# An attention and feed-forward kernel on one core: a written-out order for the first bodies on every engine, one semaphore for each batch's row maxima, and the adapter's first product in two column halves

## What is computed

```python
# layer 0: cross attention (16 heads of 16), masked, then a feed-forward net with ternary weights
q, k, v = norm(x) @ w_q + b_q, ctx @ w_k + b_k, ctx @ w_v + b_v
x = x + (softmax(mask(q k^T / 4)) v) @ w_o + b_o
x = x + relu(norm(x) @ Wq1 + b1) @ Wq2 + b2          # Wq = clip(round(W / mean|W|), -1, 1)
# layer 1: cross attention with valid lengths, then experts
x = x + (softmax(pad(q k^T / 4)) v) @ W_o.T
h = norm(x)                                            # for each of 8 experts: reconstruct h
e = argmin over experts of sum((relu(h @ Wd1[e]) @ Wd2[e] - h)^2)     # one expert for each batch
y = x + h @ W_base + relu(h @ Wa_down[e] + ba_down[e]) @ Wa_up[e] + biases
```

## Time and profile before

| | us |
|---|---|
| median of 3 runs | 1704.53 |
| lowest, highest | 1703.83, 1711.43 |
| the profiled execution: its time | 1706.53 |
| the profiled execution: its span, first to last instruction | 1704.7 |

### The profile page before, as it was taken

One profiled execution on the slowest core, in us unless ns is written; L12 is line 12 of the kernel. 1 busy time (PEld: TensorE's weight loads), 2 busy tenths in 40 slices (PEclk: granted clock), 3 DMA queues, 4 the chain that ended last, 5 costly groups with the idle time before them and its releaser, 6 DMA issues.

```text
span 1704.7 us, 43831 instructions
## 1 busy us (share of the span) xinstructions
PE 1554.4 (91%) x15136; PEld 1282.7 (75%) x15136; DVE 1271.5 (75%) x5086; ACT 912.5 (54%) x2465; POOL 1098.4 (64%) x1198
## 2 busy tenths in 40 slices
PE   2567999999999999999999999999999999999875
PEld 1356788888888887888888888888888888877654
DVE  6446778888777788887777888877777888876542
ACT  0133556655555566555555566555555665555532
POOL 4377777666667766667677766666677667666200
PEclk7689999999999999999999999999999999999977
DMA  8446565656566655565666555556656565643311
GB/s 194 77 74 90 83 101 98 96 95 95 96 105 96 107 94 96 94 91 95 104 104 99 95 96 99 92 94 102 106 92 103 95 96 96 94 77 55 54 29 31
DMA packets 286212, 157.23 MB, mean 92 GB/s; under 512 B 38820, under 2 KB 281640, under 8 KB 285992
## 3 DMA queue, kind: packets, MB, share of 16 engines
q1 hardware_dynamic: 285992, 154.44, 56.0%
HBM read 111.36 MB, written 41.96 MB: 90 GB/s over the span
## 4 chain that ended last, share of the span: by engine, by line
PE 45%; DVE 24%; DMA 12%; issue 9%; SPq 7%; POOL 2%; ACT 1%; POOLq 0%; DVEq 0%; ACTq 0%
DMA qs<-scr 10%; DVE dif L924 7%; DVE dump L858 7%; PE psD L1234 6%; PE psD L1223 6%; SPq L375 4%; PE psS L1165 4%; PE psD L1202 4%; PE psD L1139 4%; PE psD L1268 3%; PE psD L1215 3%; PE psX L1177 3%; PE psD L1244 3%; SPq L359 2%; PE psV L1190 2%
## 5 line engine op out<-in xcount | busy, mean ns | idle before, releaser
L629 ACT ACTIVATE pT<-psX 128x512 f32<-128x512 f32 x512 | 304.9, 595 | 289.4 <-PE psX L1177 289.2
L522 POOL TENSOR_TENSOR pT<-pT,keep 128x512 f32<-128x512 f32 x256 | 318.6, 1271 | 5.5 <-ACT pT L629 5.5
L507 POOL TENSOR_SCALAR xn<-xr,mv,rstd 128x256 f32<-128x256 f32 x256 | 311.4, 1224 | 10.1
L481 POOL TENSOR_SCALAR veps<-mv 128x2 f32<-128x2 f32 x128 | 29.2, 228 | 405.6 <-DVE mv L803 403.1
L1165 PE MATMUL psS<-ks,qs 65*128 65x128 f16 x2048 | 203.4, 222 | 68.4 <-DMA qs<-scr 50.4
L850 DVE TENSOR_REDUCE mx<-psS 128x4 f32<-128x512 f32 x256 | 173.9, 679 | 119.4 <-PE psS L1165 119.4
L858 DVE CUSTOM_DVE_ANT_0 dump<-psS,bias 128x128 bf16<-128x128 f32 x1024 | 234.1, 285 | 34.2 <-PE psS L1165 31.6
L673 ACT ACTIVATE dif<-dif 128x256 f32<-128x256 f32 x512 | 208.6, 411 | 49.8 <-DVE dif L924 47.9
L924 DVE SCALAR_TENSOR_TENSOR dif<-psD,bd2s,xT 128x256 f32<-128x256 f32 x512 | 213.7, 471 | 21.1 <-PE psD L1244 21.1
L1177 PE MATMUL psX<-qs,ks 67*128 67x128 f16 x2048 | 199.7, 219 | 28.8 <-DMA qs<-mrows 18.5
L1165 PEld LDWEIGHTS psS<-ks,qs 65*128 65x128 f16 x2048 | 136.8, 98 | 114.9 <-issue 70.6
(11 more groups left out here) (103 smaller groups left out, 3006.7 us busy)
## 6 DMA issues: line engine op xcount, KB each, us to landing
scr<-packed SPq DMA_DIRECT2D x128, 256.0 KB, 2.4
ks<-scr SPq DMA_DIRECT2D x256, 128.0 KB, 5.3
qs<-scr SPq DMA_DIRECT2D x256, 128.0 KB, 4.4
adapter<-in_adapters SPq DMA_DIRECT2D x64, 192.5 KB, 3.7
xr<-in_x SPq DMA_DIRECT2D x32, 256.0 KB, 2.8
ctxT<-in_ctx SPq DMA_DIRECT2D x32, 256.0 KB, 3.0
qs<-mrows SPq DMA_DIRECT2D x512, 2.0 KB
out_y<-xr SPq DMA_DIRECT2D x32, 256.0 KB, 7.2
```

What stands on the lines that cost most here:

```text
L507: nc.gpsimd.tensor_scalar(xn[:, XN[s], b], xr[:, p % NX, b], mv[:, s, b, 0:1], rstd[:, s, b:b + 1], ALU.subtract, ALU.mult).then_inc(norme ...
L522: nc.gpsimd.tensor_tensor(blk, blk, keep[:, p % 2, j // 4].unsqueeze(1).to_broadcast([P, 4, P]), ALU.mult).then_inc(masked.sem, 1)
L629: nc.scalar.activation(pT[:, j], X[:], ACT.Exp, scale=SCALE).then_inc(exp_done[l].sem, 1)
```

## The change

**The slots.** A body has 96 slots instead of 16, so that each call has a slot of its own, and the loops begin at slot 220 (2.3 bodies). What comes before, the head, is written out call by call on each engine. Behind the head the order on each engine is the one of before, with one exception: `down` stands ahead of `scores_t(0, p, 5)` instead of behind `scores(1, p, 3)`, and `a_relus` ahead of `exps(0, p, 5)` instead of behind it. The waits of `normalise` and `exps` for who used their buffer last no longer come from a formula: they look into a table `holder` of the last user.

**The semaphores.** `m_landed` becomes one for each batch.

**The product.** `down` takes 64 of the adapter's columns instead of 128 (the upper 64 held nothing that was read), and the second batch's result goes to partitions 64 to 127. `a_relus` reads it there.

```diff
-BODY = 16
-LATE_SLOT = -4
-GAMMA_SLOT = -6
-QUANT_SLOT = -2
-FIRST = -14
-END = BODY * (NP - 1) + 83
+BODY = 96
+HEAD_END = 220
+TAIL_BEGIN = BODY * (NP - 1) + 462
...
-        m_landed = [sem(f"m_landed{l}") for l in range(2)]
+        m_landed = [[sem(f"m_landed{l}{b}") for b in range(PB)] for l in range(2)]
...
@@ SyncE
+            load_late(0)
...
+            load_late(13)
+            spill(0, 1, 0)
+            load_late(14)
+            load(2)
+            stack(0, 1, 0)
+            spill(0, 0, 0)
+            spill(0, 1, 1)
+            stack(0, 0, 0)
+            stack(0, 1, 1)
+            load(3)
...
@@ GpSimd
-                if s in (0, 1):
-                    T_ready[s + 2].done(pool, p - 3)
-                    T_ready[s].done(pool, p - 1)
-                else:
-                    T_ready[s - 2].done(pool, min(p + 2, NP - 1))
-                    T_ready[s].done(pool, p - 1)
+                if (XN[s], b) in holder:
+                    stage, pair = holder[XN[s], b]
+                    T_ready[stage].done(pool, pair)
+                holder[XN[s], b] = (s, p)
...
+            mask_parts(0)
+            mask_bias(0)
+            rstd_of(0, 0)
+            normalise(0, 0, 0)
+            normalise(0, 0, 1)
+            weight_sums()
+            mask_parts(1)
+            add_bias(0, 0)
...
+            rstd_of(1, 0)
+            normalise(1, 0, 0)
+            normalise(1, 0, 1)
+            apply_mask(1, 1)
+            apply_mask(1, 2)
+            apply_mask(1, 3)
+            add_bias(1, 0)
+            h_lows(0, 0)
+            apply_mask(1, 4)
+            h_lows(0, 1)
+            h_lows(0, 2)
+            h_lows(0, 3)
...
@@ ScalarE
-                    nc.scalar.activation(aT[0:R, b * P:b * P + P], bank["down"][0:R, b * P:b * P + P], ACT.Relu,
-                                         bias=adapter[0:R, b, AW - 1:AW]).then_inc(a_relu.sem, 1)
+                    nc.scalar.activation(aT[0:R, b * P:b * P + P], bank["down"][R * b:R * b + R, b * P:b * P + P],
+                                         ACT.Relu, bias=adapter[R * b:R * b + R, b, AW - 1:AW]).then_inc(a_relu.sem, 1)
...
@@ VectorE
+            statistics(0, 0)
+            any_of(0)
+            weight_parts()
+            length_rows()
+            any_rows(0)
+            low(0, 1, 0)
+            statistics(0, 1)
+            quantise_all()
+            low(0, 0, 0)
...
@@ TensorE
-                for b in range(PB):
-                    for k in range(KD):
-                        ins = nc.tensor.matmul(dst[:, b * P:b * P + P], adapter[:, b, k * R:k * R + P],
+                for k in range(KD):
+                    for b in range(PB):
+                        ins = nc.tensor.matmul(dst[R * b:R * b + R, b * P:b * P + P], adapter[:, b, k * R:k * R + R],
                                                xT3[:, p % 2, k, b * P:b * P + P], start=(k == 0), stop=(k == KD - 1))
```

More of the change, by code:

```diff
@@ new lines, in _ @@
+            load_late(14)
[6 more added lines that the diff above has]
+            load(3)
+            spill(0, 1, 2)
+            spill(0, 0, 1)
+            stack(0, 1, 2)
+            stack(0, 0, 1)
+            maxima(0, 0, 0)
+            maxima(0, 0, 1)
+            maxima(0, 1, 0)
+            spill(0, 0, 2)
+            stack(0, 0, 2)
+            spill(1, 1, 0)
+            maxima(0, 1, 1)
@@ L406, in _ @@
                     store(p)
-                for p in at(t, 51):
+                for p in at(t, 287):
                     maxima(1, p, 1)
[L409 to L434, removed]
@@ L532, in _ @@
                     normalise(2, p, 0)
-                for p in at(t, 33):
+                for p in at(t, 186):
                     normalise(2, p, 1)
[L535 to L561, removed]
@@ L966, in _ @@
             dve.wait_ge(consts_ready, 4)
-            for t in range(FIRST, END):
-                for p in at(t, 64):
+            statistics(0, 0)
[7 more added lines that the diff above has]
+            low(0, 0, 0)
+            any_of(1)
+            low(0, 1, 1)
+            any_rows(1)
+            values0(0)
+            low(0, 1, 2)
+            statistics(0, 2)
@@ L1276, in _ @@
             pe.wait_ge(bq_steps, 9)
-            for t in range(FIRST, END):
-                for p in at(t, 64):
-                    reconstruct(p, 1)
+            keys(0, 0)
+            count(0)
+            values(0, 0)
+            turn(0, 0)
+            keys(0, 1)
+            queries(0, 0)
+            count(1)
+            keys(0, 2)
+            values(0, 1)
+            turn(0, 1)
+            queries(0, 1)
+            scores(0, 0, 0)
+            scores(0, 0, 1)
+            count(2)
@@ new lines, in _ @@
+            turn(0, 2)
+            scores(0, 0, 2)
+            scores(0, 0, 3)
+            scores(0, 0, 4)
+            scores(0, 0, 5)
+            scores(0, 0, 6)
+            scores(0, 0, 7)
+            scores_t(0, 0, 0)
+            scores(0, 1, 0)
+            scores_t(0, 0, 1)
+            scores_t(0, 0, 2)
+            scores(0, 1, 1)
+            scores_t(0, 0, 3)
+            scores(0, 1, 2)
+            scores_t(0, 0, 4)
+            scores(0, 1, 3)
+            scores_t(0, 0, 5)
@@ new lines, in _ @@
+            mix(0, 0, 0)
+            scores_t(0, 0, 6)
+            scores(0, 1, 4)
+            scores_t(0, 0, 7)
+            scores(0, 1, 5)
+            scores_t(0, 1, 0)
+            mix(0, 0, 1)
+            scores(0, 1, 6)
+            queries(0, 2)
+            output(0, 0)
+            keys(1, 0)
+            scores(0, 1, 7)
+            scores_t(0, 1, 1)
+            scores_t(0, 1, 2)
+            values(0, 2)
+            turn(1, 0)
+            scores_t(0, 1, 3)
+            ffn_up(0, 0)
@@ new lines, in _ @@
+            scores_t(0, 1, 4)
+            mix(0, 1, 0)
+            ffn_up(0, 1)
+            ffn_up(0, 2)
+            scores(0, 2, 0)
+            ffn_up(0, 3)
+            scores_t(0, 1, 5)
+            scores(0, 2, 1)
+            scores(0, 2, 2)
+            scores(0, 2, 3)
+            scores_t(0, 1, 6)
+            ffn_down(0, 0)
+            scores(0, 2, 4)
+            scores_t(0, 1, 7)
+            ffn_down(0, 1)
+            scores(0, 2, 5)
+            mix(0, 1, 1)
+            output(0, 1)
```

807 lines of the change are left out of this document (510 added, 297 removed).

## The result

| | before | after |
|---|---|---|
| median us | 1710.2 (6 runs) | 1723.47 (6 runs) |
| lowest, highest | 1703.83, 1712.84 | 1718.98, 1731.11 |
| profiled span | 1704.7 | 1722.3 |

The ratio is 1.0098, with an interval of 1.0079 to 1.0118: the change makes the kernel slower, by 17 us, where I expected 4 us less. The forecast had the two effects right in sign and place, and the wrong one of them larger. The medians of the table lie 13.3 us apart, the profiled executions (1706.53 and 1724.15) 17.6; the 17 us are the ratio's. The median of before is 5.7 us above the 1704.53 that the forecast's 1700.5 was counted from, so 5.7 of the 23 us between 1700.5 and 1723.47 have nothing to do with the change.

The account below looks back on a forecast made before the run. TensorE was taken to bound the steady bodies, with 41 us lost at the start. From the profiled 1706.5, minus 16 (head), minus 1 (tail), plus 13 (steady bodies) gave 1702.5, a median near 1700.5; range 1687 to 1712.

Parts of the forecast that it names:

- the two effects: Head written out gains 16 us at the start; moved `down` and `a_relus` lose 13 us in the steady bodies.
- Part 1: Start of the head: first scores come at 50 us, 12 us later than before; bounds 45 to 53.
- Part 2: Head from first scores to `keys(0, 3)`: that step comes at 121 instead of 137.4, gaining 16 us; bounds 10 to 22.
- The later segments: Head: `output(0, 0)` to `turn(1, 0)` 10 us, then 13 to `ffn_down(0, 0)`, then 18 to `keys(0, 3)`.
- Part 3: Steady bodies: sixth `scores_t` waits 0.46 us longer for the exponential, 28 times, 13 us lost; bounds 0 to 26.
- T: Steady body: moment when the last `queries` has issued and `scores_t(0, p, 5)` could start; sixth product forecast at T + 1.86.
- Part 4: The rest: maxima's semaphores and buffer holders cost 0; the last `down` in the tail saves 1 us.
- B: Steady bodies: the stall at the sixth product is absorbed by other waits, 1687.5 us; chance 0.15.
- C: Steady bodies: halves run one after the other or drain costs 0.4 us or more, loss 26, 1713.5 us; chance 0.10.
- D: Head brings nothing: first scores after 60, `keys(0, 3)` near 137 again, 1716.5 us; chance 0.10.
- E: Steady bodies: saved product time counts in full, new order costs nothing, 13 us more gain, 1674.5; chance 0.05.
- the head's bound of 10: Head's lowest gain, 10 us, if first scores come at 53 and later waits for spills come back.

Follow-up runs that it names:

- experiment 1: Changed kernel with `down` and `a_relus` back at their old places, new head and column halves kept: 1702.06 us, ratio 0.9959.
- 8: Kernel of experiment 1 with SyncE issuing pair 1's queries' stack, then the first maxima, ahead of pair 2's keys' stack: 1699.06 us in one run.
- experiment 9: As 8, and VectorE's statistics of pair 3 moved from behind the second maximum to behind the seventh: 1697.91 us, ratio 0.995.
- experiment 3: Kernel before the change with only the column halves of `down`, at its old place: 1707.79 us, ratio 1.0002.
- experiment 6: Changed kernel with both batches' 64-column products on one column half, one after the other, `a_relus` reading partitions 0 to 63: 1727.26 us, ratio 1.012.
- 2: Kernel before the change with only `down` and `a_relus` moved ahead, old head and whole columns kept: 1729.26 us, ratio 1.0118.
- experiment 7: Changed kernel with the two activations of `a_relus` in swapped order: 1721.0 us in one run.
- experiment 10: Kernel of experiment 1 with the 15 late weight loads behind the first stack of queries: 1711.15 us in one run.

## Why the prediction was wrong

**Part 1** held in this execution, in part by luck: first scores 52.61 for 50, within its bounds of 45 to 53, but experiments 1, 8 and 9, with the same head up to there, had them at 55.36, 53.54 and 55.80. GpSimd's mask step began at 35.59, just before VectorE's last step of the quantisation ended (36.18), so the order of events was as worked out. The quantisation began at 27.75, not 1 us earlier than before (27.3), and the queries' stack was issued at 45.87 for 43 to 44.

**Part 2** failed mainly in one step, "scores of pair 1 alternate with `scores_t` of pair 0 with no DMA wait between ... `output(0, 0)` at 80". I counted the eight score steps as 13 us and let the first `scores_t` follow. It needs the maxima of the first batch, and these go through `split_max`, SyncE's queue, and a DMA: 19.1 us from the first scores to the first `scores_t`, 6 more than I had. SyncE issued these maxima at 65.21, 3.4 us after they were ready (61.80), behind two stacks, and they landed by 71.70, when the product started. That is 6.5 us from issue to use. In before the maxima of the second batch went out at 55.33 and were used at 59.12, 3.8 us later. The DMA engines were hardly busy then (share 0.02), and 0.84 busy in the stretch of after. First before, then after, in the columns of the earlier trace rows; the last three are TensorE's granted clock, the DMA share and GB/s:

```profile
55.33:59.12 3.79, 0.01 (x1) 0.04 (x2) 1.40 (x4) 0.17 (x1) 2.15 (x2) 0.50 0.02 2
65.21:71.70 6.49, 0.61 (x5) 0.35 (x5) 2.32 (x19) 0.00 (x0) 1.46 (x2) 0.50 0.84 78
```

My sum had no term for what the loads, spills and stacks of later pairs, which now stand ahead of these maxima, do to them. How much of the 6 us is the queue's, the busy DMA engines' or the clock's no run took apart. The rest, to `output(0, 0)`, was 19.1 instead of 17; the first `mix` ran at the low level of the clock (granted 0.50 from 78.90 to 80.90) and took 1.94 us, for 1.08 in before at the full clock (granted 1.00 from 64.40 to 66.00). The later segments came out at 7.5 (10), 11.8 (13) and 18.5 (18); the first of them shrank by 2.6 us though I had said that nothing shortens it. A wait for the turned maxima was in before too, for those of the second batch:

```profile
59.12 0.59 PE L1177 MATMUL psX<-qs,ks 67*128 67x128 f16 x4 [4.25 <-DMA qs<-mrows]
```

My rows left it out.

**Part 3** had the mechanism, the place, the engine and the number of times right, and the size wrong: 0.46 us a body, measured 0.83 to the sixth product and 0.88 in the period, and 24 us in all for 13. Two terms of it were off:

- "`a_relus` to T + 1.22": the pair was priced at 0.52, the row of the whole-column product; on two partition halves it is 0.78. That is 0.26 of the 0.36 us missing (experiments 3 and 6). The edit changed the partitions that ScalarE reads, and I carried the duration over without a bound.
- "`down` ends at T + 0.48 + 0.16": it ended at T + 0.75, and `a_relus` began at T + 0.79 for T + 0.70; 0.09 us. The changes of tiling show in the rows: with whole columns (2) `down` starts 0.11 us after the last `queries` product and holds TensorE for 0.89, with 64 columns one after the other (6) it is 0.20 and 1.02. So a body seems to pay 0.09 on the way in and 0.13 on the way out, 0.22 in all (the 0.13 supposes that the eight records themselves take as long on 64 columns as on 128, which no run shows; what does show is that the weight loads idle 0.17 us behind `down` in the timeline of after), and the halves save 0.21 us of TensorE's row (1.00 to 0.79), not 0.47. The Trainium skill's rule in TensorEngine Tiling (Array Packing), Key Properties, that a change of mode drains the array, agrees with this in kind; the loss by it, 17 us with my 0.2, was nearer than my 13, for the smaller of the two reasons.

**Part 4** held: 1.12 us for 2.08 in the tail, and no new wait at the maxima's semaphores in steady bodies.

**The rivals.** B (absorbed) is refuted: the two DMA waits kept 14.7 of their 16.1 us. C had the right side and nearly the size of a body's loss (0.9; its 1713.5 took 17 us of gain for granted), by the wrong cause: the halves do overlap (experiment 6) and the changes of tiling cost 0.22 together by the reading above. D is refuted, `keys(0, 3)` is 8.8 us earlier; E is refuted by experiment 3. With both sizes as measured the sum is 1706.5 - 8 - 1 + 24 = 1721.5, against 1724.15 of the profiled execution; most of the remaining 2.6 us come behind `down(27)`, from 16.6 us late there to 18.7 at `down(31)`. The range had no place for both sizes being off the same way: I had given each its bounds, and 0.1 to C, when the head's bound of 10 and a loss of 0.9 a body together gave 1719.5.

**Open.** GpSimd's mask step stands behind the all-reduces with 7.51 us of idle time that the profile puts down to nothing, in before 6.90; the same order on the chip twice (after and experiment 1) has its count product at 37.87 and 40.48. Half of that difference is there from the start (the first `keys` product is at 13.95 and 15.24). No run here took this apart. It bounds how well any kernel's head can be told from another's.

**The version that beats both** keeps the new head and leaves `down` and `a_relus` behind: experiments 1 (0.9959) and 9 (0.995), each 0.4 to 0.5% below before. The column halves can stay or go.

## What to carry to other kernels

A call between two uses of a single buffer pays for itself by covering the other engine's work on that buffer: move it only after writing down the whole chain that frees the buffer, on both engines, and do not count a saving in it. When an edit changes the partitions or the tile shape of an operation, give its old duration a bound of its own on every engine that touches the result, not only on the one that was made faster. In a sum for a start-up, every product that reads something which came over a DMA gets that DMA's chain as a term, from its place in the issuing queue on; the wait of before at that product is the first row to look for.

## What the hardware showed

- ScalarE: two activations of 64 x 128 take 0.52 us when both read partitions 0 to 63, and 0.78 when the second reads 64 to 127, at 0.36 us for a single one in both cases; with the order swapped the pair is as long, but the next activation starts 0.12 us earlier (experiment 7).
- TensorE: `down` on 64 columns starts 0.09 us later behind a product on 128 than on whole columns does (0.20 for 0.11), and on one half it holds TensorE 0.13 us longer (1.02 for 0.89); two column halves beside each other save 0.43 of 1.02 us.
- SyncE: 15 late weight loads take 14 to 15 us of its row; in experiment 10 those of two DMAs (`wd1s`, `bd2s`) take 2.7 us each. In experiment 9 a stack waited 6.8 us for the spill that it reads.
- DMA: four DMAs of row maxima took 6.5 us from issue to use in after, where the DMA share was 0.84, and 3.8 in before, where it was 0.02.
